# Two carry columns between the runs of a pair, and one product moved from VectorE to GpSimd

## The reference, cut to what matters

```
def _selective_scan(x, dt, Bc, Cc, A, D):
    def step(h, inp):
        x_t, dt_t, B_t, C_t = inp
        dA = jnp.exp(dt_t[:, :, None] * A)
        h = h * dA + (dt_t * x_t)[:, :, None] * B_t[:, None, :]
        y = jnp.einsum('bdn,bn->bd', h, C_t)
        return (h, y)
...
    y_f = _branch(x, conv_w_f, conv_b_f, W_xproj_f, W_dt_f, dt_bias_f, A_log_f, D_f)
    y_b = _branch(x[:, ::-1, :], conv_w_b, conv_b_b, W_xproj_b, W_dt_b, dt_bias_b, A_log_b, D_b)[:, ::-1, :]
    y = (y_f + y_b) * jax.nn.silu(z)
```

## Time and profile before

| | us |
|---|---|
| median of 3 runs (20558.29 to 20561.16) | 20560.99 |
| the profiled execution, its own time | 20586.68 |
| its span, first to last instruction | 20584.9 |
| mean granted TensorE clock | 0.928 |

### The profile page before, as it was taken

The page is one execution under the profiler, slowest core; times in us unless marked ns, Lnnn a source line. Parts: engine busy times, 40 slices in busy tenths (PEclk is TensorE's granted clock), DMA queues, the critical chain, the costliest instruction groups (busy, mean ns, idle before and its releaser), DMA issues. The chain is left out here.

```text
span 20584.9 us, 179901 instructions
## 1 busy us (share of the span) xinstructions
PE 17720.7 (86%) x43392; PEld 7706.0 (37%) x43392; DVE 17704.0 (86%) x14031; ACT 14006.9 (68%) x35077; POOL 17627.3 (86%) x10484
## 2 busy tenths in 40 slices
PE   7888988888888888888988888888898888888888
PEld 3433433334343343333433334333343333433334
DVE  7988979889798897988979789797997979979799
ACT  5757757577675776757767577676776757767577
POOL 6978969789797897979979799697997979979799
PEclk9989989899898998989989899898998989989899
DMA  2313313133131332313323133231332323323233
GB/s 83 132 63 126 134 73 132 63 127 134 73 132 63 126 134 74 131 63 126 134 75 131 63 129 129 75 131 66 132 123 75 132 73 131 118 74 132 70 133 119
DMA packets 528855, 2178.88 MB, mean 106 GB/s; under 512 B 96328, under 2 KB 243424, under 8 KB 527648
## 3 DMA queue, kind: packets, MB, share of 16 engines
q1 hardware_dynamic: 527648, 2165.99, 29.0%
HBM read 1905.47 MB, written 245.63 MB: 104 GB/s over the span
## 5 line engine op out<-in xcount | busy, mean ns | idle before, releaser
L1026 DVE TENSOR_TENSOR_SCAN arena<-ps,arena 128x897 f32<-128x897 f32 x5376 | 10977.2, 2064 | 1051.0 <-ACT arena L1182 718.4
L1234 POOL TENSOR_TENSOR arena<-arena 128x896 f32<-128x896 f32 x5376 | 9978.7, 1874 | 621.5 <-PE ps L956 524.0
L956 PE MATMUL ps<-arena,ident 128*128 128x448 f32 x21504 | 9142.6, 562 | 1141.1 <-POOL arena L1234 1141.0
L1166 ACT ACTIVATE ps<-arena,A 128x448 f32<-128x448 f32 x10752 | 6412.1, 632 | 2128.7 <-DVE arena L1026 2097.6
L956 PEld LDWEIGHTS ps<-arena,ident 128*128 128x128 f32 x21504 | 4050.3, 194 | 5882.2 <-issue 3545.5
L1226 POOL TENSOR_TENSOR arena<-arena 128x896 f32<-128x896 f32 x2240 | 4678.9, 2089 | 0.0
L1015 DVE TENSOR_TENSOR arena<-ps,arena 128x896 f32<-128x896 f32 x3136 | 3338.7, 1065 | 30.4 <-ACT ps L1128 30.4
L913 PE MATMUL ps<-arena,diag 128*128 128x448 f32 x5376 | 2199.3, 553 | 116.6 <-issue 114.6
L913 PEld LDWEIGHTS ps<-arena,diag 128*128 128x128 f32 x5376 | 1031.7, 194 | 1197.4 <-issue 1110.6
L1215 POOL TENSOR_TENSOR arena<-arena 128x448 f32<-128x448 f32 x672 | 758.4, 1137 | 455.4 <-DVE arena L995 455.4
L1182 ACT ACTIVATE arena<-arena 128x2 f32<-128x2 f32 x5376 | 1041.2, 194 | 53.3 <-DVE arena L1026 53.3
(11 more groups left out here) (160 smaller groups left out, 20216.6 us busy)
## 6 DMA issues: line engine op xcount, KB each, us to landing
arena<-bc_rows SPq DMA_DIRECT2D x1792, 896.0 KB, 5.1
x_projected<-arena SPq DMA_DIRECT2D x112, 672.0 KB, 3.5
y_forward<-arena SPq DMA_DIRECT2D x112, 672.0 KB, 3.6
arena<-x_projected SPq DMA_DIRECT2D x112, 672.0 KB, 7.7
arena<-y_forward SPq DMA_DIRECT2D x112, 672.0 KB, 4.1
x<-in_x SPq DMA_DIRECT2D x119, 336.0 KB, 3.6
x_normed<-arena SPq DMA_DIRECT2D x112, 336.0 KB, 2.8
arena<-x_normed SPq DMA_DIRECT2D x112, 336.0 KB, 4.2
```

Of the source, the lines that this page charges most:

```text
L956: m = e.matmul(y, ident[:, :], pr[:, q % NPR, a * T:a * T + T], start=False, stop=p == NP - 1 and a == 1)
L1026: e.tensor_tensor_scan(rev(hh[:, q % NH, 0:W2], s), rev(decays(q)[:, 0:W2], s), rev(bb[:, q % NB, 0:W2], s), car[:, k, n:n + 1] if i % NC ...
L1166: e.activation(two(decays(q))[:, a, :], dt[:, r % NDT, :], ACT.Exp, scale=Am[s][:, k, 2 * p + a:2 * p + a + 1]).then_inc(c_ex, 1)
L1234: e.tensor_tensor(pr[:, q % NPR, :].rearrange("p (a b) -> p a b", a=2), two(hh[:, q % NH, :]), cr[:, 2 * p:2 * p + 2, :], ALU.mult).then_i ...
```

## The change

The gap between the two runs of `bb`, `hh` and the decays grows from one column to two, so that both runs begin at even columns of `arena`; the scan is 898 columns long in place of 897. Forward the second of the two columns is the carry's, backward (where the scan runs from the end) the first; the other column holds zeros in `bb`, set once an image by three small memsets. And pair 7 of row 0 is moved from VectorE's products to GpSimd's.

```diff
-W2 = 2 * T + 1
+T2 = T + 2
+W2 = 2 * T + 2
...
-ON_VECTOR = [[0, 1, 0, 1, 1, 0, 1, 1], [0, 1, 0, 1, 1, 0, 1, 0], [0, 1, 1, 0, 1, 0, 1, 1]]
+ON_VECTOR = [[0, 1, 0, 1, 1, 0, 1, 0], [0, 1, 0, 1, 1, 0, 1, 0], [0, 1, 1, 0, 1, 0, 1, 1]]
...
-    bb = take(NB, 2 * T1)
-    hh = take(NH, 2 * T1)
+    bb = take(NB, 2 * T2)
+    hh = take(NH, 2 * T2)
...
-        return ps[:, b:b + 2, :].rearrange("p a b -> p (a b)")[:, 0:2 * T1]
+        return ps[:, b:b + 2, :].rearrange("p a b -> p (a b)")[:, 0:2 * T2]
...
-                        w.wait_ge(c_pad, 1)
+                        w.wait_ge(c_pad, NB + 1)
...
+        for k in range(NB):
+            e.memset(bb[:, k, T:T2], 0.0).then_inc(c_pad, 1)
         e.memset(xh[0][:, :, 0:3], 0.0).then_inc(c_pad, 1)
         for b in DECAY:
-            e.memset(ps[:, b, T:T1], 0.0)
+            e.memset(ps[:, b, T:T2], 0.0)
...
+            w.wait_ge(c_pad, NB)
...
-            e.activation(bb[:, q % NB, T:T1], car[:, k, n:n + 1] if i % NC else zero[:, 0, 0:1],
+            e.activation(bb[:, q % NB, T + 1 - s:T2 - s], car[:, k, n:n + 1] if i % NC else zero[:, 0, 0:1],
...
-            e.activation(car[:, k, 2 * p:2 * p + 2], h[:, 0:T1 + 1:T1] if s else h[:, T - 1:W2:T1],
+            e.activation(car[:, k, 2 * p:2 * p + 2], h[:, 0:T2 + 1:T2] if s else h[:, T - 1:W2:T2],
```

## The result

The changed kernel takes 20866.4 us (median of 4 runs, 20864.3 to 20881.8) against 20561.1: ratio 1.0148, 95% interval 1.0135 to 1.0160. It is slower by 305 us.

The account below looks back on a forecast made before the run. GpSimd was taken to set the pace except at TensorE waits; 5.6 + 8.0 + 5.7 = 19.3 us an image, x 16 = +309 us, gave 20870 us (+1.5%), range 20700 to 21030.

Parts of the forecast that it names:

- What an output costs: Outputs on GpSimd: one run slow, one fast, 1.927 us each, +0.053 on the mean, +17.9 us an image.
- The distance rule: On GpSimd, distance from first input to second, modulo 4 columns: 0 or 3 slow (2.086 us), 1 or 2 fast (1.767).
- Rivals 1 and 2: Outputs: second run alone decides, all 1.767 us, 20340 (chance 0.08); first run alone, all 2.086, 21680 (chance 0.04).
- The terms: GpSimd, per image: outputs +17.9 us, moved product +28.6, together 46.5; VectorE's scan +0.8, hidden by idle time.
- What the waits give: GpSimd's waits for TensorE absorb added work, leaving 19.3 us an image: forward 5.6, backward 8.0, first and last backward chunks 5.7.
- Rival 3: GpSimd's waits give nothing, since TensorE slips with it: the full +744 us, 21305; chance 0.04.
- the two short stretches: Two short waits in most chunks, in row 1, set by TensorE; outside them GpSimd sets the pace.
- the 15 outputs: Forward, outputs up to the next TensorE stretch: 15 x 0.159 - 5 x 0.319 = +0.8 us a chunk, 5.6 in seven.
- rival 1: All outputs fast at 1.767 us, second run alone decides; forward -1.6 us a chunk, in all -219, 20340; chance 0.08.

Follow-up runs that it names:

- every operation fast: hh buffers 900 columns apart, 2 more unused columns in front of dt, B and zs, against the kernel before: 20054.6 us, ratio 0.9762.
- the kernel before with every output fast: hh buffers 900 columns apart in place of 898, one carry column and its own product table kept, against the kernel before: 20256.6 us, ratio 0.9860.

## Why the prediction was right

It forecast 20870 us, +309; 20866 and +305 were measured. Point by point:

**What an output costs.** The forecast 1.927 is the measured 1.929. The distance rule behind it was read from six lines of the trace and now has direct tests: both inputs moved, nothing changes; one pair of inputs moved apart, the class changes, as it does for the normalisation products; order swapped, the sign shows; distances 3, 2, 1 side by side, slow, fast, fast. That the price is the sum over the runs is shown by slow then fast (the changed kernel) and by the swapped inputs (2, 3 and 0, 1), all at 1.93. Rivals 1 and 2, where one run alone decides, are out. Why the chip behaves so is not shown; only the period of 4 columns, 16 bytes, and the sign are.

**The terms.** GpSimd's added work was put at 46.5 us an image, and is 46.1. The scan was to be 2 ns longer and is 5, still hidden: VectorE had 107 us of idle time over the scans of an image. The product kept its 2.09.

**What the waits give.** I put 27 of the 46.5 us there and 26.6 were found. The reasoning on place is borne out by the pair of runs that move one product each (94 against 439 us). Forward, in the third image, the chunk shown grew by 1.36 us, over the 0.8 forecast. Backward, the chunk shown grew by 1.92 (1.6 to 1.75 forecast), the first by 3.48 and the last by 3.16 (2.8 and 2.9). Rival 3, the waits give nothing, would have been +744.

On average over all images the seven forward chunks grew by 5.0 us together (5.6 forecast), the seven backward ones by 14.7 (13.7 forecast), so the sum came out close because two small errors have opposite signs. Most of the second is in the first and the last backward chunk, 6.6 us together on average where 5.7 were forecast. In the forward chunk shown row 0 took 2.46 us more and row 1 1.10 less; the excess over the forecast is a wait of 0.57 us for ACT ahead of the normalisation products, which was not there before:

```profile
3126.73 1.92 POOL L1213 TENSOR_TENSOR arena<-arena 96x448 f32<-96x448 f32 x2 [0.57 <-ACT arena L1071]
```

Most other forward chunks don't have it.

**What it had wrong.** I took "GpSimd has no gap" as "GpSimd sets the pace" outside the two short stretches. Row 2 of the forward chunk shows otherwise. It took 23.51 us before, 23.51 in the changed kernel and 23.51 with every operation fast, here in that order, each from its own kernel's profile:

```profile
3127.90:3151.41 23.51, 20.98 (x47) 8.04 (x46) 22.51 (x18) 19.31 (x49) 23.48 (x14) 0.93 0.67 248
```

```profile
3163.01:3186.52 23.51, 19.70 (x47) 7.59 (x46) 22.52 (x17) 19.31 (x49) 23.51 (x14) 1.00 0.61 239
```

```profile
3051.99:3075.50 23.51, 20.60 (x49) 8.23 (x50) 22.51 (x17) 19.32 (x50) 21.62 (x14) 1.00 0.67 250
```

VectorE is busy for 22.51 of it, and the rest is one wait for ACT in each of the three kernels; in the last it is this one:

```profile
3063.00 0.62 DVE L999 TENSOR_TENSOR arena<-arena,ps 128x448 f32<-128x448 f32 x1 [1.00 <-ACT ps L1128]
```

So in that row two limits coincided, which is part of why the kernel with everything fast fell short of -640. The eight outputs there (+0.42 us together) are not free for that: GpSimd only falls further behind. Output 96, the first of the next row 0, starts 2.78 us after the end of its scan before and 3.33 in the changed kernel, and the scans of that row wait for it. With the columns alone the first six forward chunks took 0.72 us more in row 0, on average over all images, and nothing more in rows 1 and 2. So the 15 outputs count as forecast, but the row in which the time shows is not the row in which the work was added. Work taken away from GpSimd is another matter: forward, rows 1 and 2 give nothing back.

The price of rival 1 is wrong for the same reason. It had every forward chunk 1.6 us shorter with all outputs fast, and next to nothing backward; the kernel before with every output fast gained 0.7 a chunk forward and 1.7 backward. No run has all outputs fast together with the moved product alone, so the 20340 stays untested.

The estimate of 1.12 us for a VectorE product, by the Trainium skill ("Vector Engine (DVE) Microarchitecture Reference", §5.2), used a figure that the page gives for both sources at odd words, while here both sources begin at even columns and only the output's second run is odd. The 1.065 us speaks against carrying the figure over to the output, not against the figure.

## What to carry to other kernels

When one instruction of a kind has two durations, group it by what repeats (here the buffer number) before taking its mean: the mean of 1874 hid a choice of layout worth 288 us on the outputs and 489 on all operations. Set the columns of a GpSimd operation's two inputs against each other, not each against zero, and look at what else a shift moves; the unused columns, 14 at most, showed no cost here. And before work is moved to the busiest engine, look which wait stands behind the place: one product cost 94 us in front of a wait and 439 behind it. An engine without gaps may still not set the pace of that stretch, and a run that makes it faster tells. And where a difference is small, take the changed stretch by itself: the rest of this kernel varied by up to 6 us an image with the same work.

## What the runs showed of the hardware that was not expected

A GpSimd operation on two 32-bit inputs of 896 columns took 2.09 us where the second input began 0 or 3 columns after the first, modulo 4, and 1.77 where it began 1 or 2 after it; with 448 columns 1.13 to 1.14 and 0.93 to 0.98, and an operation with one run of each kind took 1.93. Where the output lies showed no influence: products took 2.09 whichever `bb` they wrote, with the second run at an odd or an even column, and outputs kept 1.93 when `pr` moved by 2. Swapping the two factors of a product, which changes nothing in the result's definition, changed the kernel's time by 136 us. A product of VectorE took 1.064 to 1.066 us whether the second run of its output began at an odd or an even column.
